# Token attention with its value operand made from x and the token keys first, and the probabilities as the stationary operand

## The reference

```
query, keyt, valt = x @ Wq, enc @ Wk, enc @ Wv          # enc: the 2044 other context rows
hs      = mha(query, keyt, valt)                        # 8 heads of 80
ca_q1   = einsum('btc,th->bch', ca, Wq_ca)[:, indices]  # 384 distinct rows, spread to 1024
ca_hs1  = mha(ca_q1, x, x)
ca_q2   = ca_hs1 @ Wq
ca_hs2  = mha(ca_q2, ca @ Wk_ca, ca @ Wv_ca)            # keys and values: the 4 tokens
out     = (hs + ca_hs2) @ Wout + b_out + x
```

## Time and profile before

| | |
|---|---|
| median of 3 runs | 1215.27 us (1214.89 to 1215.36) |
| the profiled execution's own time | 1215.66 us |
| its span | 1213.8 us |
| `project` on PE | about 7 to 275 us |
| `tokens` on PE | about 275 to 424 us |
| granted TensorE clock in `tokens` | 1.00 |

### The profile page before, as it was taken

How to read it: one execution, slowest core, us unless ns; L and a number is a source line. 1 busy time by engine, 2 the same in 40 slices (tenths; PEclk the granted TensorE clock), 3 DMA queues, 4 the chain that set the end, 5 groups by cost and what they waited for, 6 DMA issues and landing times.

```text
span 1213.8 us, 14595 instructions
## 1 busy us (share of the span) xinstructions
PE 1201.0 (99%) x5660; PEld 908.1 (75%) x5660; DVE 824.5 (68%) x1179; ACT 681.6 (56%) x784; POOL 206.0 (17%) x117
## 2 busy tenths in 40 slices
PE   7999999999999999999999999999999999999999
PEld 6888888787666667777777777777777777776899
DVE  6458625761144378888888888888888888885551
ACT  5323433223644377677777677677777777778310
POOL 0100000010000021222221221221221221221233
PEclk9999999999999999999999999999999999999999
DMA  8975785693910074254344344335335325422254
GB/s 297 347 276 174 260 298 209 232 319 120 301 16 1 1 196 98 87 132 110 98 121 110 109 120 112 106 111 126 100 102 145 96 87 153 125 73 66 70 218 148
DMA packets 77936, 178.09 MB, mean 147 GB/s; under 512 B 14169, under 2 KB 31705, under 8 KB 74026
## 3 DMA queue, kind: packets, MB, share of 16 engines
q1 hardware_dynamic: 70106, 156.29, 42.2%
q0 software_dynamic: 2864, 10.24, 2.6%
q10 hardware_dynamic: 4896, 10.62, 2.6%
HBM read 113.72 MB, written 63.24 MB: 146 GB/s over the span
## 4 chain that ended last, share of the span: by engine, by line
PE 99%; ACT 0%; DMA 0%; issue 0%; DVE 0%; ACTq 0%
PE at_ps L1281 30%; PE bank L698 20%; PE at_ps L1262 20%; PE at_ps L234 9%; PE acc_t_ps L1055 7%; PE at_ps L1469 6%; PE s_ps L1023 2%; PE bank L645 1%; PE bank L675 1%; PE f_ps L998 1%; PE acc_t_ps L1034 1%; PE f_ps L234 1%; PE f_ps L977 1%; PE f_ps L987 0%; PE at_ps L1472 0%; DMA ctx_f<-in_ctxT 0%
## 5 line engine op out<-in xcount | busy, mean ns | idle before, releaser
L250 DVE TENSOR_REDUCE mpart<-at_ps 128x1 f32<-128x512 f32 x480 | 325.3, 686 | 99.8 <-PE at_ps L234 99.7
L1202 ACT ACTIVATE prob_hi<-at_ps 128x1024 fp32r<-128x1024 f32 (+1 forms) x256 | 263.0, 1027 | 188.9 <-PE at_ps L1262 188.9
L1281 PE MATMUL at_ps<-prob_hi,v 128*81 128x512 f32 (+1 forms) x1024 | 317.1, 395 | 0.2 <-issue 0.2
L1139 DVE TENSOR_TENSOR prob_lo<-probs,prob_hi 128x1024 fp32r<-128x1024 f32 (+1 forms) x211 | 271.7, 1288 | 24.0 <-ACT probs L1207 23.4
L1207 ACT ACTIVATE probs<-at_ps 128x1024 f32<-128x1024 f32 (+1 forms) x256 | 261.3, 1021 | 0.0
L1281 PEld LDWEIGHTS at_ps<-prob_hi,v 128*81 128x81 f32 (+1 forms) x1024 | 150.5, 149 | 69.6 <-issue 6.2
L1139 POOL TENSOR_TENSOR prob_lo<-probs,prob_hi 128x1024 fp32r<-128x1024 f32 x45 | 108.0, 2401 | 514.2 <-ACT probs L1207 514.2
L234 PE MATMUL at_ps<-a 128*128 128x512 f32 x480 | 188.1, 392 | 0.0
L1262 PE MATMUL at_ps<-a 128*128 128x512 f32 (+1 forms) x512 | 160.0, 394 | 1.2 <-ACT probs L1207 0.6
L1262 PE MATMUL at_ps<-b 113*128 113x512 f32 (+1 forms) x512 | 161.1, 396 | 0.0
L1281 PE MATMUL at_ps<-prob_lo,v 128*81 128x512 f32 (+1 forms) x512 | 160.3, 394 | 0.0
(11 more groups left out here) (149 smaller groups left out, 1392.8 us busy)
## 6 DMA issues: line engine op xcount, KB each, us to landing
v_hi_d<-v_t SPq DMA_DIRECT2D x16, 648.0 KB, 5.8
v_lo_d<-v_t SPq DMA_DIRECT2D x16, 648.0 KB, 7.1
v<-v_hi_d SPq DMA_DIRECT2D x16, 648.0 KB, 4.8
v<-v_lo_d SPq DMA_DIRECT2D x16, 648.0 KB, 6.0
k_hi_d<-out_hi SPq DMA_DIRECT2D x40, 256.0 KB, 5.9
k_lo_d<-out_lo SPq DMA_DIRECT2D x40, 256.0 KB, 6.3
a<-k_hi_d SPq DMA_DIRECT2D x16, 640.0 KB, 7.6
b<-k_hi_d SPq DMA_DIRECT2D x16, 640.0 KB, 11.2
```

The costliest lines, as they stand in the source:

```text
L250: dve.tensor_reduce(self.mpart[:, g % 2, qt, c:c + 1], at[:, 0:w], AX, ALU.max).then_inc(self.mx_done, 1)
L1139: eng.tensor_tensor(pl[n % PB][0:r, :], prob[n % PF][0:r, :], ph[n % PB][0:r, :].bitcast(F32), ALU.subtract).then_inc(sem, 1)
L1202: act.activation(ph[n % PB][0:r, :], s_ps[n % 2][0:r, :], ACT.Exp, scale=SCALE).then_inc(ph_done, 1)
L1281: mm = pe.matmul(o_ps[:, u * CH:(u + 1) * CH], a[0:r, t, :], y[n % PB][0:r, u * CH:(u + 1) * CH], start=t == 0 and m == 0, stop=t == KT - ...
```

## The change

The product of probabilities, x and folded keys is taken in another order. First x is multiplied by the folded token keys of all heads: for each tile of 128 rows of x that is 5 matmuls with a 128 x 128 block of x stationary and 64 or 96 columns of keys moving (`key_sums`, L85 of the changed kernel). The result, `y`, holds 32 columns and 2 of ones per head. Then in each step the probabilities are stationary, three blocks of 128 columns, and 64 columns of `y` move (L1118), and the sum over 4 steps is what `token_scores` gave before. So `raw_out`, `token_scores`, `fold_keys` and the copy of x with ones fall away, and `fold` waits for the last step of its head.

The folded keys of both batches and `y` of batch 1 are made within `project`: new jobs `t` (Wk_ca by tokens), `w` (that by Wq, L750, 25 matmuls of 128 stationary and 64 moving columns) and `y` (4 jobs) stand among the last `k` and `v` jobs of batch 1. `y` of batch 0 is made in steps 12, 15, 18 and 21 of `tokens`. All of these are in fp32. The job list now runs through both batches without a break.

```diff
-FOLD_AT = {0: (0, 1, 2), 1: (3, 4, 5), 2: (6, 7), 3: (8, 9)}
+FOLD_AT = {1: (0, 1), 2: (2, 3), 3: (4,)}
+Y0_AT = {12: 0, 15: 1, 18: 2, 21: 3}
+YC = HT + 2
+YW = 64
+EXTRA_AT = {("k", 0): ("t", 0), ("k", 1): ("t", 1), ("k", 2): ("t", 2), ("k", 4): ("w", 0),
+            ("v", 3): ("y", 0), ("v", 4): ("y", 1), ("v", 5): ("y", 2), ("v", 6): ("y", 3)}
+TOKEN_GROUPS = ((0, 1), (2, 3), (4,))
...
+def heads_of(m):
+
+    first, last = (range(m * P, (m + 1) * P)[i] // D for i in (0, -1))
+    return first, last + 1, sum(heads_of(i)[1] - heads_of(i)[0] for i in range(m))
+
+
+def key_sums(pe, to, x, w2, t):
+
+    for m in range(MC):
+        first, end, at = heads_of(m)
+        mm = pe.matmul(to[:, t % 2, first * HT:end * HT], x[:, m, t * P:(t + 1) * P],
+                       w2[:, at * HT:(at + end - first) * HT], start=t % 2 == 0 and m == 0,
+                       stop=t % 2 == 1 and m == MC - 1, skip_group_check=True)
+    return mm
...
+                if (b, c) == (B - 1, NS - 1) and (job[0], i) in EXTRA_AT:
+                    kind, m = EXTRA_AT[job[0], i]
+                    jobs.append((b, kind, c, m))
...
-                        sp.dma_start(kept["wqT"][:], d["wqT"].rearrange("(m p) n -> p m n", p=P)
-                                     ).then_inc(kept["wqT_in"], 16)
-                        x1 = d["x_ones"].rearrange("b (t p) (h d) -> b p t h d", p=P, d=DA)[B - 1]
-                        for t in range(ST):
-                            sp.dma_start(kept["xn1"][:, t], x1[:, t]).then_inc(kept["xn1_in"][t // 2], 16)
-                        for name in ("wkca", "caT", "mask", "wvca"):
-                            sp.dma_start(kept[name], d[name].rearrange("(m p) n -> p m n", p=P)
-                                         ).then_inc(kept["small_in"], 16)
...
+                    for name in ("wkca", "caT", "mask"):
+                        sp.dma_start(kept[name], d[name].rearrange("(m p) n -> p m n", p=P)
+                                     ).then_inc(kept["small_in"], 16)
+                    sp.dma_start(kept["wqT"][:], d["wqT"].rearrange("(m p) n -> p m n", p=P)
+                                 ).then_inc(kept["wqT_in"], 16)
+                    sp.dma_start(kept["xT"], xT[:, b]).then_inc(kept["xT_in"], 16)
+                    sp.dma_start(kept["wvca"], d["wvca"].rearrange("(m p) n -> p m n", p=P)
+                                 ).then_inc(kept["wvca_in"], 16)
...
+            def token_keys(bank, i):
+
+                first, n = TOKEN_GROUPS[i][0], len(TOKEN_GROUPS[i])
+                dve.tensor_copy(kept["tok0"][:, first:first + n], bank[:, 0:n * B * NT].rearrange(
+                    "p (m t) -> p m t", m=n)).then_inc(done, 1)
+                if i < len(TOKEN_GROUPS) - 1:
+                    return
+                dve.wait_ge(kept["small_in"], 48)
+                dve.wait_ge(done, extra["t", i] + 1 + 8)
+                for b in range(B):
+                    dve.tensor_tensor(kept["bd0"][:, :, b], kept["tok0"][:, :, None, b * NT:(b + 1) * NT].to_broadcast(
+                        [P, MC, NH, NT]), kept["mask"][:, :, :, None].to_broadcast([P, MC, NH, NT]), ALU.mult
+                        ).then_inc(bd_done, 1)
+
+            def key_blocks(bank, _):
+
+                for m in range(MC):
+                    first, end, at = heads_of(m)
+                    for b in range(B):
+                        mm = dve.tensor_tensor(
+                            kept["w2"][b][:, at * HT:(at + end - first) * HT].rearrange("p (h n) -> p h n", n=HT),
+                            bank[:, None, (m * B + b) * HT:(m * B + b + 1) * HT].to_broadcast([P, end - first, HT]),
+                            kept["mask"][:, m, first:end, None].to_broadcast([P, end - first, HT]), ALU.mult)
+                        mm.then_inc(*((done, 1) if (m, b) == (MC - 1, B - 1) else (w2_done, 1)))
+
+            def key_rows(bank, i):
+                dve.tensor_copy(kept["y1"][:, 2 * i:2 * i + 2, :, 0:HT],
+                                bank[:].rearrange("p (t h n) -> p t h n", t=2, h=NH)).then_inc(done, 1)
...
+                if kind == "t":
+                    if m == 0:
+                        pe.wait_ge(kept["small_in"], 48)
+                    for i, group in enumerate(TOKEN_GROUPS[m]):
+                        mm = fold_tokens(pe, kept, "wkca", bank[:, i * B * NT:(i + 1) * B * NT], group)
                     mm.then_inc(full, 1)
+                    continue
...
+                if kind == "w":
+                    pe.wait_ge(kept["wqT_in"], 16)
+                    pe.wait_ge(bd_done, B)
+                    for r in range(MC):
+                        for k in range(MC):
+                            mm = pe.matmul(bank[:, r * B * HT:(r + 1) * B * HT],
+                                           kept["wqT"][:, k, r * P:(r + 1) * P],
+                                           kept["bd0"][:, k].rearrange("p b h t -> p (b h t)"),
+                                           start=k == 0, stop=k == MC - 1)
+                    mm.then_inc(full, 1)
...
+                if kind == "y":
+                    if m == 0:
+                        pe.wait_ge(kept["xT_in"], 16)
+                        pe.wait_ge(w2_done, B * MC - 1)
+                        pe.wait_ge(done, extra["w", 0] + 1 + 8)
+                    to = bank[:].rearrange("p (t n) -> p t n", t=2)
+                    for t in (2 * m, 2 * m + 1):
+                        mm = key_sums(pe, to, kept["xT"], kept["w2"][b], t)
+                    mm.then_inc(full, 1)
...
-            sp.dma_start(kept["wk2"][:], d["wk2_frame"]).then_inc(wk2_in, 16)
+            sp.dma_start(xT, d["xT"].rearrange("b (m p) s -> p b m s", p=P)[:, 0]).then_inc(xT_in, 16)
             sp.dma_start(eye_f[:], d["eye"]).then_inc(eye_in, 16)
-            sp.wait_ge(wk2_full, 1)
+            at.load_a(sp, scratch, 0)
             sp.dma_start(wout[:], rows(d["wout"])).then_inc(wout_in, 16)
...
-            def raw_out(n):
-                act.wait_ge(pv_done, (n + 1) * pairs)
-                if n >= 2:
-                    act.wait_ge(t_full, n - 1)
-                act.activation(raw[n % 2][:], acc_ps[n % 2], ACT.Copy).then_inc(raw_done, 1)
...
+                at = beside(h)[1]
+                dve.wait_ge(pv_done, (n + 1) * pairs)
+                chained(dve.reciprocal(rden[:, n % 2, :], t_ps[n % 2][:, :, at + HT]))
...
-                if n and j == 2:
+                if n and j == 0:
                     fold(n - 1)
                     if n == NH:
                         center(order[0])
                     if n == NH + 1:
                         weigh(0, order[0])
+                if k in Y0_AT:
+                    i = Y0_AT[k]
+                    dve.wait_ge(y_full, i + 1)
+                    dve.tensor_copy(y[0][:, 2 * i:2 * i + 2, :, 0:HT],
+                                    f_ps[i % 2][:].rearrange("p (t h n) -> p t h n", t=2, h=NH)).then_inc(y_done, 1)
...
-            def fold_keys():
-                pe.wait_ge(wqT_in, 16)
-                pe.wait_ge(bd_done, 4 * B)
-                for h in range(NH):
-                    for m in range(MC):
-                        mm = pe.matmul(f_ps[0][0:D, h * B * HT:(h + 1) * B * HT], wqT[:, m, h * D:(h + 1) * D],
-                                       bd[0][:, m].rearrange("p b h t -> p (b h t)"),
-                                       start=m == 0, stop=m == MC - 1)
-                mm.then_inc(wk2_full, 1)
...
+            def key_pair(i):
+                if i == 0:
+                    pe.wait_ge(xT_in, 32)
+                    pe.wait_ge(tok_done, 1)
+                if i >= 2:
+                    pe.wait_ge(y_done, i - 1)
+                to = f_ps[i % 2][:].rearrange("p (t n) -> p t n", t=2)
+                for t in (2 * i, 2 * i + 1):
+                    mm = key_sums(pe, to, xT, w2[0], t)
+                mm.then_inc(y_full, 1)
...
-            def token_scores(n):
-                b, h = heads[n]
-                if n == 0:
-                    pe.wait_ge(wk2_done, B)
-                pe.wait_ge(raw_done, n + 1)
-                for c in range(KC):
-                    mm = pe.matmul(t_ps[n % 2][:, c, :], raw[n % 2][:, c * P:(c + 1) * P],
-                                   kept["wk2"][:, b, h, :], start=True, stop=True)
-                mm.then_inc(t_full, 1)
...
-                if n == 0 or (b == 0 and h == 0):
-                    pe.wait_ge(xn_in[b][j], 32)
...
-                    pe.wait_ge(raw_done, n - 1)
                     pe.wait_ge(step, folded(n - 2))
                 for t in range(2):
-                    mm = pe.matmul(acc_ps[n % 2], xn[b][:, 2 * j + t, h, :], p1[k % 3][:, t, :],
-                                   start=j == 0 and t == 0, stop=j == pairs - 1 and t == 1)
+                    own = y[b][:, 2 * j + t].rearrange("p h n -> p (h n)")[:, beside(h)[0]:beside(h)[0] + YW]
+                    for c in range(KC):
```

(59 more changed lines are left out.)

448 lines of the change are left out of this document (217 added, 231 removed).

## The result

The changed kernel takes 1333.23 us (median of 4 runs, 1332.33 to 1336.38) against 1215.08 for the kernel before (4 runs): ratio 1.0976, 95% interval 1.0959 to 1.0992. It is 118 us slower. The prediction said 1225.8, with a range of 1221 to 1231.

The account below looks back on a forecast made before the run. PE, busy for 99% of the span at 2.4 GHz, was taken as the bound. Terms 3.8 - 10.8 - 5.7 + 5.6 + 17.9 gave +10.8 us, taken as +10.5 on 1215.3: 1225.8 us, range 1221 to 1231.

Parts of the forecast that it names:

- The clock falls: Rival in the steps of `tokens`: PE held by loads drops to 1.2 GHz, +22 to +109 us, 1248 to 1335 us; 3 in 100.
- `fold_tokens`: Term: its Wk_ca half moves to `project` with the same records, priced at 0.
- The pace follows the moving columns: Rival for the added records: 64 moving columns run at 0.071 us each, -29 us, 1186 us; 4 in 100.
- Job `w`: Term in `project`: 25 matmuls, 50 records with 128 stationary columns, +5.6 us.
- `y` jobs: Term, half in `project`, half in steps 12 to 21: 160 records, +17.9 us; each job over 2.2 us.
- `project`: Sign in the profile after: this stage ends some 18 us later.
- `tokens`: Sign in the profile after: this stage gets shorter by about 7 us.
- Edits at no cost: Copies, loads and moved operations beside PE's work add nothing; all these waits together bounded at 0 to 5 us.
- The cover of `fold`: `fold` waits for its head's last values; PE needs it 4 steps later, over 6 us, so no wait.

Follow-up runs that it names:

- b32: Kernel before, its 384 moving columns of probabilities cut into twelve matmuls of 32, x loaded anew for each: 1593.41 us (one execution).
- fold128: Changed kernel, with the 30 token-value records of steps 1 to 3 moving 128 columns instead of 8: 1225.09 us, ratio 1.0079.
- mix_wide_narrow: Changed kernel, with 128 columns of y moving for batch 1, which comes first, and 64 for batch 0: 1224.98 us (one execution).
- w128: Changed kernel, with 128 instead of 64 columns of y moving in each value matmul: 1224.31 us, ratio 1.0073.
- fold_spread: Changed kernel, with the five groups of token-value records spread over steps 1, 3, 4, 6 and 7 instead of 1 to 3: 1329.10 us (one execution).
- burst_wide: Changed kernel, with 128 columns of y in every step and the token values made three times over in step 2 (90 records of 8 columns): 1240.47 us.
- b64: Kernel before, its 384 moving columns cut into six matmuls of 64, x loaded anew for each: 1257.96 us (one execution).
- fold_each: Changed kernel, with one group of 6 token-value records in each of steps 0 to 4: four runs of 1224.13 to 1224.86 us, two of 1333.92 and 1336.37.
- mix_narrow_wide: Changed kernel, with 64 columns of y moving for batch 1, which comes first, and 128 for batch 0: 1279.62 us (one execution).
- head0_narrow_rep: Changed kernel, with 64 columns of y moving in the first head (steps 0 to 3) and 128 in all others, repeated: 1229.75 us (4 runs).

## Why the prediction was wrong

**The step that failed is the clock: every term of the sum was priced at 2.4 GHz, and the rival "The clock falls" was put at 3 in 100.** In its place the runs show 1.2 GHz from 301 to 533 us, with steps of 3.20 and 3.63 us. The mechanism and a price up to 1335 us were on the page; the chance was read wrongly, from one row. The prediction leaned on L987 having kept 2.4 GHz for 5.7 us "where loads set the pace". But L987 streams 64 columns, 0.053 us, in each 0.071, and the new records stream the same 0.053 in each 0.112. Of the rows with few moving columns it was the less like the change: in b32 the low clock even came up within L987. The row to ask was L977, 8 columns in 0.112 us, which in the kernel before stood 12 or 18 at a time between records of 384 columns, and in the changed kernel between records of 64. That edit, the neighbours of `fold_tokens`, was priced at 0 because its own records stay the same.

The Trainium skill, "TensorE: Matmul & The Clock Gate", Part 1, says that the clock is set by how busy PE has been recently. In this case's trace that can't be read from the busy rows: matmul and load rows were busy for 6.98 of the 7 us before the fall and for all of 301 to 308 us.

**The size.** The clock is worth 1333.2 - 1225.1 = 108 us, the difference to fold128, which differs in the width of 30 records. A step with a row maximum takes 3.63 us for 1.92, a plain one 3.20 for 1.69, and 20 records of `y` in `tokens` 4.24 (334.98 to 339.22 us) for 2.21 (319.03 to 321.24 in fold128). With those 108 us away, the rest is +9.8 us by fold128's median, of +10.8 summed and +10.5 forecast. That the rival's upper price of 1335 us came so near is partly luck. It took 1.7 us more in all 64 steps; the clock was low in 61, of which 32 have a row maximum and cost 1.71 more and 29 cost 1.51, and the 8 us that the four groups of `y` cost more, which it left out, make up for most of that.

**The terms at 2.4 GHz**, read from fold128 and from the two kernels:

- *The pace follows the moving columns* (4 in 100) was wrong, as argued: 12 records and two scores of 64-column steps take 1.69 us (411.94 to 413.63 us in mix_wide_narrow), predicted 1.70, and w128 has the same time with twice the columns.
- *Job `w`*: 50 records in 5.50 us from its start to that of the next job (267.58 to 273.08), predicted 5.6. *`y` jobs*: 2.15 us each, predicted 2.2. The end of each group hides a load, as the prediction said it might.
- *`project`* ends 17.4 us later (first scores at 292.6 us, before 275.2), predicted 18. *`tokens`* from the first values to `fold_values` takes 421.12 - 294.04 = 127.1 us, and in the kernel before 411.59 - 276.65 = 134.9 us: 7.9 us shorter, predicted about 7.
- *Edits at no cost* held: PE has no wait for `w2`, x or `y`; its only wait there is the 0.55 us at the first step, as before. The cover of `fold`, put at over 6 us, ran out only in fold_spread, by 2.4 us and once.

**What is shown and what is not.** Shown: the fall is brought by records with few moving columns under a long load (after against w128 and fold128, b32, burst_wide), not by the order of the product, not by the probabilities being stationary, not by DMA traffic. Shown: the 64-column steps of the changed kernel keep the level that they find; in b64, where the loads are of 80 columns, such steps brought the clock back. Shown: near the edge the program alone doesn't settle the outcome (fold_each fell in 2 of 6 runs on one chip). Not shown: what differs between such executions, and whether 96 columns keep the level each time, as there is one run of them. No version here beats the kernel before: at the upper clock the change costs 978 load-paced records and saves 432 (256 of them long), and the best form, w128 or fold128, is 0.7 to 0.8% slower.

## What to carry to other kernels

Before splitting a matmul or swapping its operands, write down for each record its load and its stream; where the load is the longer one over a long stretch, PE's rows can look full while its clock is halved, and then the terms nearly double (1.92 to 3.63 us here). If such a stretch is needed, let more columns move, up to the load's length: here, at 2.4 GHz, it cost nothing, and it was worth 108 us. Look at what stands between the thin records after the change as well as at the records themselves, and repeat a kernel near this edge several times before trusting one reading.

## What the runs showed of the hardware that was not expected

The granted clock fell from 2.4 to 1.2 GHz without a gap in PE's rows in the 7 us before, and stayed for 232 us of steps that, entered from a wide step, ran at 2.4 GHz. From the low level it came back in the first wide step of mix_narrow_wide and in the second of head0_narrow_rep and burst_wide. At the low level the loads slow down with the array: the records of burst_wide, some 0.11 us apart at first, are (2.50 - 0.36)/10 = 0.214 us apart at the low level (11 records from 302.82 us), and a LDWEIGHTS row of 128 columns lasts 326 ns in the mean of L1118 against 187 to 192 in fold128.
